# Turning the next batch's normalised rows on VectorE and ScalarE instead of TensorE, in a four-stage conditional-residual kernel

## What is computed

```python
def _L0_cond_ref(x, lang, W1, b1, W2, b2, gamma, beta):
    h = relu(einsum('bsh,bha->bsa', x, W1[lang]) + b1[lang])
    adapted = einsum('bsa,bah->bsh', h, W2[lang]) + b2[lang]
    x = x + adapted
    mean = mean(x, -1); var = mean(square(x - mean), -1)
    normed = (x - mean) * rsqrt(var + 1e-5)
    return normed * gamma[lang] + beta[lang]

x = x + _L0(...)      # adapter, layer norm
x = x + _L1(...)      # x @ weight[subj].T + bias
x = x + _L2(...)      # five feed-forward nets 256 -> 1024 -> 256 (two experts, three shared), gated
x = x + _L3(...)      # masked softmax pooling over the 512 rows
```

## Time and profile before

| | |
|---|---|
| time, median of 3 | 500.68 us (500.46 to 500.73) |
| profiled execution, its own time | 501.22 us |
| span in that profile | 499.4 us |
| PE busy | 493.0 us, 99% |
| PE weight loads | 407.7 us, 82% |
| DVE busy | 348.8 us, 70% |
| ACT busy | 260.3 us, 52% |
| POOL busy | 236.0 us, 47% |
| granted TensorE clock | 0.998 of full |

### The profile page before, as it was taken

How to read it: one execution, slowest core, us unless ns; L and a number is a source line. 1 busy time by engine, 2 the same in 40 slices (tenths; PEclk the granted TensorE clock), 3 DMA queues, 4 the chain that set the end, 5 groups by cost and what they waited for, 6 DMA issues and landing times.

```text
span 499.4 us, 6992 instructions
## 1 busy us (share of the span) xinstructions
PE 493.0 (99%) x2320; PEld 407.7 (82%) x2320; DVE 348.8 (70%) x702; ACT 260.3 (52%) x506; POOL 236.0 (47%) x201
## 2 busy tenths in 40 slices
PE   8999999999999999999999999999999999999996
PEld 5787888888888888888888888888888888888985
DVE  5587235885688799786478689788568779644467
ACT  4655555543457574444446656454345757445243
POOL 1575446445264446444544447444525444746023
PEclk9999999999999999999999999999999999999999
DMA  5865354322255443422227454422222342331002
GB/s 154 185 185 150 101 147 147 100 85 85 85 120 145 116 115 87 127 85 84 85 85 169 123 161 123 132 84 85 85 85 85 100 112 84 88 131 37 0 1 84
DMA packets 77657, 52.97 MB, mean 106 GB/s; under 512 B 40758, under 2 KB 67382, under 8 KB 77622
## 3 DMA queue, kind: packets, MB, share of 16 engines
q1 hardware_dynamic: 75734, 50.44, 35.5%
q10 hardware_dynamic: 1888, 2.10, 1.3%
HBM read 48.33 MB, written 2.10 MB: 101 GB/s over the span
## 4 chain that ended last, share of the span: by engine, by line
PE 90%; DVE 5%; DMA 3%; issue 1%; ACT 0%; ACTq 0%; DVEq 0%; SPq 0%
PE ps_hid L839 14%; PE ps_hid L840 14%; PE ps_hid L844 14%; PE ps_net L901 13%; PE ps_net L896 13%; PE ps_net L897 13%; DMA raw_wo<-in_L_cond_share_wo_dram 3%; PE ps_net L868 2%; DVE pick L1680 1%; DVE hid_lo L1827 1%; PE ps_side L537 1%; PE ps_side L541 1%; PE ps_side L536 1%; PE ps_side L547 1%; PE ps_side L550 1%
## 5 line engine op out<-in xcount | busy, mean ns | idle before, releaser
L1924 POOL TENSOR_TENSOR wi_lo<-raw_wi,wi_hi 128x512 fp32r<-128x512 f32 x77 | 101.6, 1319 | 207.5 <-ACT wo_hi L1088 110.2
L1109 ACT ACTIVATE hid_hi<-ps_hid 128x512 fp32r<-128x512 f32 x160 | 95.5, 598 | 194.1 <-PE ps_hid L844 192.3
L1827 DVE SCALAR_TENSOR_TENSOR hid_lo<-ps_hid,hid_hi 128x512 fp32r<-128x512 f32 x160 | 109.8, 688 | 113.9 <-ACT hid_hi L1109 112.5
L839 PE MATMUL ps_hid<-x2T_hi,wi_lo 128*128 128x512 f32 (+1 forms) x332 | 125.9, 381 | 0.0
L840 PE MATMUL ps_hid<-x2T_hi,wi_hi 128*128 128x512 f32 (+1 forms) x332 | 125.3, 379 | 0.0
L896 PE MATMUL ps_net<-hid_hi,wo_hi 128*128 128x512 f32 x304 | 118.9, 391 | 0.0
L897 PE MATMUL ps_net<-hid_hi,wo_lo 128*128 128x512 f32 x304 | 118.5, 390 | 0.0
L1925 POOL TENSOR_TENSOR wo_lo<-raw_wo,wo_hi 128x512 fp32r<-128x512 f32 x77 | 104.1, 1352 | 0.0
L844 PE MATMUL ps_hid<-x2T_lo,wi_hi 128*128 128x512 f32 (+1 forms) x332 | 98.9, 379 | 0.0
L901 PE MATMUL ps_net<-hid_lo,wo_hi 128*128 128x512 f32 x304 | 94.0, 390 | 0.3 <-DVE hid_lo L1827 0.3
L839 PEld LDWEIGHTS ps_hid<-x2T_hi,wi_lo 128*128 128x128 f32 x332 | 62.4, 188 | 11.9 <-POOL wo_lo L1925 0.2
(11 more groups left out here) (329 smaller groups left out, 500.1 us busy)
## 6 DMA issues: line engine op xcount, KB each, us to landing
raw_wi<-in_L_cond_share_wi_dram SPq DMA_DIRECT2D x23, 512.0 KB, 3.8
raw_wo<-in_L_cond_share_wo_dram SPq DMA_DIRECT2D x23, 512.0 KB, 4.8
raw_wi<-in_L_cond_expert_wi_dram SPq DMA_DIRECT2D x16, 512.0 KB, 3.8
raw_wo<-in_L_cond_expert_wo_dram SPq DMA_DIRECT2D x16, 512.0 KB, 4.8
next_x2T<-in_x_dram SPq DMA_DIRECT2D x24, 64.0 KB, 4.3
x_rows<-in_x_dram SPq DMA_DIRECT2D x3, 512.0 KB, 4.1
x_rows<-netT SPq DMA_DIRECT2D x48, 32.0 KB, 2.0
out_dram<-out_rows SPq DMA_DIRECT2D x5, 256.0 KB, 5.7
```

The source lines that it names most:

```text
L839: mm(dst, wi_lo[:, w, k, c], x2T_hi[:, k, rows], start=(k == 0), stop=False)
L1109: fn(hid_hi[:, ring(b, q)], ps_hid[:, ring(b, q)], ACT.Relu).then_inc(hid_hi_ready, 1)
L1827: v.scalar_tensor_tensor(out=hid_lo[:, ring(b, q)], in0=ps_hid[:, ring(b, q)], scalar=0.0, in1=f32(hid_hi[:, ring(b, q)]), op0=ALU.max, op ...
L1924: g.tensor_tensor(wi_lo[:, w], raw_wi[:, half % 2, :, c], f32(wi_hi[:, w]), ALU.subtract)
```

## The change

The four transposes a slot on PE go. DVE turns the 32x32 blocks of `norm` in place of them (two instructions, slot 30), which leaves each block turned but in its old place: block (a, c) of each 128x128 square must then go from partition group a to partition group c. ACT carries them, in slots 30 to 33: in slot 30 + a it reads partitions 32a to 32a+31 and writes the four partition groups c = 0 to 3 one after the other, each copy 32 partitions x 256 elements (8 runs of 32). So there are 16 copies a batch. `normT` is then an SBUF tile (`x1T`), DVE makes `x1T` from it in slot 33, and `x1_hi` does both halves in slot 34. To make room, the steps ahead stand one slot earlier: `w2`, `subj_blocks` 24, `hid` 25, `subj_w` 26, `adapt` 27, `stats` 28, `xb` and `norm` 29. `subj_wT` moves from `norm` to `next_x2T`, so that `adapt` need not wait for `subj_w_lo`. Slots of `x1_lo`, `y` and `base` stay.

```diff
-    A_SLOT = dict(w1=20, blocks=20, xT=22, w2=25, subj_blocks=25, hid=26, subj_w=27, adapt=28, stats=29, xb=31, norm=30, normT=32, x1_hi=33, x1_lo=35, y=36, base=37)
+    A_SLOT = dict(w1=20, blocks=20, xT=22, w2=24, subj_blocks=24, hid=25, subj_w=26, adapt=27, stats=28, xb=29, norm=29, turn=30, x1=33, x1_hi=34, x1_lo=35, y=36, base=37)
...
-        subj_blocks, subj_wT = subj_w, norm[:, 0:KD]
+        subj_blocks, subj_wT = subj_w, next_x2T[:, :, 0:D]
+        norm_blocks, normT = next_x2T, x1T
...
-                        else:
-                            pe.wait_ge(a_dve.sem, a_dve.at(i, "subj_w_lo"))
...
-            def normalised(slot, i):
-                if 0 <= slot - A_SLOT["normT"] < KD:
-                    k = slot - A_SLOT["normT"]
-                    pe.wait_ge(a_dve.sem, a_dve.at(i, "norm"))
-                    for r in range(R):
-                        last = nc.tensor.transpose(ps_side[:, k, r * P:(r + 1) * P], norm[:, r, k * P:(k + 1) * P], ident[:])
-                    last.then_inc(a_pe.sem, 1)
...
+                if 0 <= slot - A_SLOT["turn"] < P // BK:
+                    a = slot - A_SLOT["turn"]
+                    act.wait_ge(a_dve.sem, a_dve.at(i, "turn1"))
+                    for c in range(P // BK):
+                        blocks = norm_blocks[a * BK:(a + 1) * BK].rearrange("p k (r s) -> p k r s", s=P)[:, :, :, c * BK:(c + 1) * BK]
+                        cols = normT[c * BK:(c + 1) * BK].rearrange("p k (r s) -> p k r s", s=P)[:, :, :, a * BK:(a + 1) * BK]
+                        last = fn(cols, blocks, ACT.Copy)
+                    last.then_inc(a_act.sem, 1)
...
+                if slot == A_SLOT["x1"]:
+                    dve.wait_ge(a_act.sem, a_act.at(i, f"turn{P // BK - 1}"))
+                    for k in range(KD):
+                        v.scalar_tensor_tensor(out=x1T[:, k], in0=normT[:, k], scalar=gamma[:, k:k + 1], in1=xbT[:, k],
+                                               op0=ALU.mult, op1=ALU.add).then_inc(a_dve.sem, 1)
...
+                if slot == A_SLOT["turn"]:
+                    here("norm")
+                    for k in range(KD):
+                        v.transpose(norm_blocks[:, k].rearrange("p (r s) -> p r s", s=P),
+                                    norm[:, :, k * P:(k + 1) * P]).then_inc(a_dve.sem, 1)
```

More of the change, by code:

```diff
@@ L276, in cond_resid_program @@
         evac_dve = Steps(sem("evac_dve"), "g0 g1 g2 g3")
-        a_pe = Steps(sem("a_pe"), "hid adapt0 adapt1 normT0 normT1 y0 y1", 1)
-        a_act = Steps(sem("a_act"), "xhi0 xhi1 hid_below hid_up subj_w_hi x1hi0 x1hi1", 1)
+        a_pe = Steps(sem("a_pe"), "hid adapt0 adapt1 y0 y1", 1)
+        a_act = Steps(sem("a_act"), "xhi0 xhi1 hid_below hid_up subj_w_hi turn0 turn1 turn2 turn3 x1hi0 x1hi1", 1)
         a_dve = Steps(sem("a_dve"), "w1_hi xT0 xT1 xlo0 xlo1 w2_hi w2_up b2_hi b2_lo subj_wT hid_sum hid_hi hid_lo subj_w_lo sum0 sum1 stats sums mean var_eps "
-                                    "norm xb0 xb1 x1T0 x1T1 x1lo0 x1lo1 x2T0 x2T1", 1)
+                                    "xb0 xb1 norm turn0 turn1 x1T0 x1T1 x1lo0 x1lo1 x2T0 x2T1", 1)
         a_pool = Steps(sem("a_pool"), "w1_lo w2_lo rstd", 1)
@@ L914, in batch @@
                         second_product(b, s, first, last)
-                    if not last:
-                        normalised(q, b + 1)
                     if not first:
@@ L951, in stage_a @@
                     fn(subj_wT_hi[:], subj_wT, ACT.Copy).then_inc(a_act.sem, 1)
[L952 to L955, removed]
+                if 0 <= slot - A_SLOT["turn"] < P // BK:
[6 more added lines that the diff above has]
+                    last.then_inc(a_act.sem, 1)
+                if slot == A_SLOT["x1_hi"]:
+                    for k in range(KD):
+                        act.wait_ge(a_dve.sem, a_dve.at(i, f"x1T{k}"))
+                        fn(opT_hi[:, k], x1T[:, k], ACT.Copy).then_inc(a_act.sem, 1)
             def stage_c(slot, i):
@@ L1270, in stage_a @@
                     last.then_inc(a_dve.sem, 1)
-                if 0 <= slot - A_SLOT["normT"] < KD:
-                    k = slot - A_SLOT["normT"]
-                    dve.wait_ge(a_pe.sem, a_pe.at(i, f"normT{k}"))
-                    here(f"xb{k}")
-                    v.scalar_tensor_tensor(out=x1T[:, k], in0=ps_side[:, k], scalar=gamma[:, k:k + 1], in1=xbT[:, k],
-                                           op0=ALU.mult, op1=ALU.add).then_inc(a_dve.sem, 1)
+                if slot == A_SLOT["turn"]:
+                    here("norm")
+                    for k in range(KD):
+                        v.transpose(norm_blocks[:, k].rearrange("p (r s) -> p r s", s=P),
+                                    norm[:, :, k * P:(k + 1) * P]).then_inc(a_dve.sem, 1)
                 if slot == A_SLOT["x1_lo"]:
```

## The result

| | before | changed |
|---|---|---|
| time, median of 5 | 500.73 us (500.46 to 501.35) | 514.41 us (513.89 to 515.13) |
| ratio | | 1.0272, 95% interval 1.0258 to 1.0286 |
| profiled execution, its own time | 501.22 us | 514.41 us |
| span of the profile | 499.4 us | 512.6 us |
| mean granted TensorE clock | 0.998 | 0.984 |

What follows compares the result with a forecast made beforehand. PE, busy 99% of the span, bounds the kernel. Three batches of 2.9 us wait less 1.0 saved give +5.7 us: 506.9 profiled, 506.4 us on the median's scale, range 502.5 to 509.4.

Steps and rivals of the forecast that it cites:

- Saved, 1.0 us a batch: On PE, slots 32 to 34 get shorter without the transposes: 1.0 us a batch, 3.0 us in all.
- The rival that a transpose is worth its 0.272 us: On PE, 24 transposes save their full duration, 6.5 us in place of 3.0, giving 502.9 us; chance 0.03.
- The stretch from the first copy to `netT`, 10.6 us: On ACT, 8.2 us with overlap everywhere, plus 20 starts on another partition group at 0.12 us each.
- The first two rivals: On ACT, copies overlap after all: 499.2 us, chance 0.09; only a new reading group waits: 500.7 us, chance 0.06.
- When the copies start, H + 3.3: ACT's first copy starts 3.3 us after H, the start of ACT's `hid_hi` of slot 30.
- DVE's statistics are done by then: On DVE, statistics end before POOL ends slot 28's weights at H - 1.2 (H: start of slot 30's `hid_hi`).
- The bound of H + 4.3: Late end for the copies' start after slot 30's `hid_hi` starts (H): a wait of 3.9 us and 509.4 us.
- the scalings meet POOL's split again: On DVE, scalings take 3.32 us, copies start 2.1 later, PE waits 5.0, time 512.7 us; chance 0.05.
- When PE asks, H + 11.0, and where it waits: PE reaches bank 0 in slot 34 11.0 us after slot 30's `hid_hi` starts (H), waiting 2.9 us for `netT`.
- Nothing gives this back: PE's 2.9 us wait in slot 34, in the middle of a product, is not recovered later.
- What a wait costs: its own length.: PE's wait in slot 34 was counted at its length alone, 2.9 us a batch.
- `adapt`, `hT_both`, `x1T`, `y` at nothing: Slots 27 and 33 to 36: data arrives in time, no cost; 0.1 to 0.3 us a batch if `adapt`'s cover is gone.

Runs made afterwards that it cites:

- Experiment 7: The changed kernel without ACT's 16 copies, `x1T` made from the turned blocks where they lie: 498.51 us, ratio 0.9943 to the kernel before.
- experiment 3: The changed kernel with each copy of slot 30 + a writing the partition group a that it reads, same count and size: 507.32 us, ratio 1.0125.
- experiment 1: The changed kernel with 14 matmuls on zeros on PE ahead of its slot 34 wait for `netT`: 509.47 us, ratio 1.0162.
- experiment 2: The kernel before, transposes kept, with 18, 30 or 60 unread ACT copies ahead of `netT` in slot 34: 502.60, 506.86 and 521.59 us.
- experiments 5 and 6: The changed kernel with `netT` ahead of slot 33's four copies: 510.84 us; the same plus six matmuls on zeros before PE's slot 34 wait: 510.44 us.
- the first kernel of experiment 2: The kernel before with 18 unread ACT copies of 128 x 32 ahead of `netT` in slot 34: 502.60 us, ratio 1.0024.
- experiment 8: The changed kernel with DVE placing all 16 blocks: 502.47 us; also `y` a slot later: 501.73 us; carrying shared between ACT and DVE: 501.70 us.

## Why the prediction was wrong, step by step

It forecast 506.4 us in a range of 502.5 to 509.4 and got 514.41: slower, as it said, but by 13.7 us in place of 5.7.

- **Saved, 1.0 us a batch**: right. Experiment 7 gave 2.4 us in the median and 1.0 to 1.1 a batch in the trace. The rival that a transpose is worth its 0.272 us is out.
- **The stretch from the first copy to `netT`, 10.6 us**: right, 10.51, and for its reason, the starts that wait for a change of group (experiment 3). The first two rivals are out.
- **When the copies start, H + 3.3**: too early. It was H + 5.07, 3.92 and 3.92. The step that failed is "DVE's statistics are done by then", read off, where no split ran beside them. The change moves the statistics from slot 29 to 28, an even slot, in which POOL splits weights; one small addition was blocked for 1.1 us. The bound of H + 4.3 allowed for one such meeting, at `xbT`. And in the first batch the rival "the scalings meet POOL's split again" came true beside it, at 1.0 us in place of 2.1, since one scaling met it and not two. The waits were 10.9 us in place of 8.7: 2.2 of the 8.0 us that are missing.
- **When PE asks, H + 11.0, and where it waits**: right; it was H + 11.23. "Nothing gives this back" too.
- **What a wait costs: its own length.** This is the step that failed most, and it was not even written as a step. Behind each wait PE ran at a granted clock of 0.50 for 4.6, 3.4 and 3.4 us, which cost 5.2 us (experiment 1; experiment 2 shows that the wait brings it). Another 0.3 a batch, 0.9 in all, go with the first matmul behind any wait, even one of 0.2 us.
- **Sum as measured**: 10.9 of waits, 5.2 of clock, 0.9 for getting going, less 3.0 saved are 14.0 us, where the slots 29 to 39 show 14.1; the medians lie 13.7 apart. Of the 8.0 us that the forecast fell short, 2.2 are the longer waits, and 6.1 are what it had at nothing; the two make 8.3, and the 0.3 over is the difference of the slots from the medians.
- **`adapt`, `hT_both`, `x1T`, `y` at nothing**: no such wait in the trace. For `y` that was luck (experiments 5 and 6).

The Trainium skill ("TensorE: Matmul & The Clock Gate", Part 1) says that the clock of an idle array falls back to 1.2 GHz. The trace agrees, with 0.50 behind the 4.4 us; a prediction that has PE standing for 3 us should have had that as a rival with a price.

What stays open: behind waits of 2.1 to 2.8 us the clock fell in some cases (2.13, 2.52, 2.52, 2.81) and in one not (2.69); it fell behind every longer one and behind none up to 1.96. So the 2.1 us that the expectation of the first kernel of experiment 2 names as harmless do not stand. Nor does the fall stand at one place: it came 2.2 us into the first wait of the change, and 1.0 and 1.4 us behind the end of the other two. And it differs between executions of one kernel: the mean granted clock was 0.984 or 0.985 in three of the change (514.41 to 515.13 us) and 0.990 in the two shortest (513.89 and 514.08), and 0.997 or 0.991 in experiment 3 (506.96 to 507.6 and 507.6 to 508.97). Nothing here tells what decides. The 5.2 us are the price in the profiled execution.

## What to carry to other kernels

Price a new wait of the busiest engine by more than its length: TensorE, having stood for 2.1 to 4.4 us in mid stream, mostly ran at half its clock for some microseconds afterwards, which added 1.3 to 2.7 us, and dead work in the gap avoided that without shortening the wait. When a change moves a chain of tiny operations by one slot, look at what the other engine on the same memory does in that slot: here an addition of four columns took 1.26 us, and the three versions of experiment 8 met the split again at other instructions. And when the first late thing is mended, look at the next deadline before counting the gain: `netT`, `y` and the gate's sum stood in line here.

## What was not expected of the hardware

- On ACT a copy whose partition group differs from that of the one ahead starts 0.01 to 0.02 us after that has ended; in the same group it starts 0.1 before (0.43 against 0.31 us from start to start, for copies of 0.41).
- The reading side seems to be kept apart for SBUF and PSUM. In slots 32 and 34 `wi_hi`, which reads SBUF from partition 0, starts 0.02 behind the end of `hid_hi`, which reads PSUM and lies on partition 0 as well; the last instruction that read SBUF was a copy from group 1 or 3. So it is in all three batches; the other 67 `wi_hi` behind a `hid_hi` in this trace start 0.1 before its end. Slot 32's is one of the prediction's twenty starts. No experiment was made on it.

```profile
110.05 0.60 ACT L1106 ACTIVATE hid_hi<-ps_hid 128x512 fp32r<-128x512 f32 x1
110.68 0.63 ACT L1078 ACTIVATE wi_hi<-raw_wi 128x512 fp32r<-128x512 f32 x1
```

- DVE's block transpose of 32 x 256 in mixed groups takes 0.436 us and steps by 0.45; the sixteen of a batch cost 7.2 us, where two of 128 x 512 turn the same data in 1.3, though they leave the blocks where they were.
- PE takes 0.3 us more behind a wait than the wait itself, from 0.2 us on.
- PE worked 2.9 to 5.8 us at the lower clock behind a wait, without a gap, before it was back at 1.00.
